# Two of sixteen query tiles of each unit folded inside the loop, three banks for maxima, four for scores

## What is computed

```python
q, k, v = (proj(wq, bq), proj(wk, bk), proj(wv, bv))      # 2 x 16 heads x 1024 x 8
scores = jnp.einsum('bhqd,bhkd->bhqk', q, k) * scale
attn = jax.nn.softmax(scores, axis=-1)
out = jnp.einsum('bhqk,bhkd->bhqd', attn, v)
...
x = layernorm(x + (out @ wo.T + bo));  x = layernorm(x + ffn(x))
```

## Time and profile before

| | |
|---|---|
| Runs | 442.76, 443.16, 443.18 us, median 443.16 |
| Profiled execution | span 441.5 us from first to last instruction |
| PE busy | 427.8 us (97%) |
| VectorE busy | 386.5 us (88%) |
| ScalarE busy | 367.7 us (83%) |
| GpSimd busy | 90.3 us (20%) |
| Granted PE clock | 1.000 on average |

### The profile page before, as it was taken

One profiled execution on the slowest core, in us unless ns is written; L12 is line 12 of the kernel. 1 busy time (PEld: TensorE's weight loads), 2 busy tenths in 40 slices (PEclk: granted clock), 3 DMA queues, 4 the chain that ended last, 5 costly groups with the idle time before them and its releaser, 6 DMA issues.

```text
span 441.5 us, 9824 instructions
## 1 busy us (share of the span) xinstructions
PE 427.8 (97%) x3496; PEld 227.0 (51%) x3498; DVE 386.5 (88%) x719; ACT 367.7 (83%) x694; POOL 90.3 (20%) x142
## 2 busy tenths in 40 slices
PE   8999999999999999999999999999899899999995
PEld 4543544444444444444444443544333488877884
DVE  6799999999999999999999999999884577657636
ACT  4487989998998999989899899999899886678762
POOL 9730000100000010000001002373311263046103
PEclk9999999999999999999999999999999999999999
DMA  6567741111130110113011001021021000000101
GB/s 165 176 196 129 270 147 33 44 28 28 48 122 25 45 31 28 27 48 122 25 46 33 26 27 49 14 43 47 15 39 50 13 8 1 1 2 2 48 1 48
DMA packets 17117, 24.88 MB, mean 56 GB/s; under 512 B 5169, under 2 KB 9009, under 8 KB 16689
## 3 DMA queue, kind: packets, MB, share of 16 engines
q1 hardware_dynamic: 16464, 23.68, 19.3%
q10 hardware_dynamic: 608, 0.59, 0.5%
HBM read 15.08 MB, written 7.60 MB: 51 GB/s over the span
## 4 chain that ended last, share of the span: by engine, by line
PE 76%; DVE 10%; ACT 5%; SPq 3%; DMA 2%; issue 2%; POOL 0%; POOLq 0%; DVEq 0%; ACTq 0%
PE ps L1369 24%; PE ps L1291 20%; PE ps L1479 16%; DVE negmax L977 9%; PE ps L1353 8%; ACT arena L664 2%; DMA parts_q<-arena 2%; PE ps L1223 2%; PE ps L1234 1%; PE ps L1423 1%; PE ps L1319 1%; PE ps L1263 1%; SPq L463 1%; SPq L435 1%; ACT v_pad L722 1%
## 5 line engine op out<-in xcount | busy, mean ns | idle before, releaser
L977 DVE TENSOR_REDUCE negmax<-ps 128x1 f32<-128x512 f32 x458 | 275.8, 701 | 1.8 <-PE ps L1291 1.5
L664 ACT ACTIVATE arena<-ps 128x512 f32<-128x512 f32 x360 | 190.0, 606 | 19.3 <-PE ps L1353 14.1
L1353 PE MATMUL ps<-qx,kx 64*128 64x512 f32 x512 | 171.3, 451 | 0.9 <-DMA qx<-mT 0.6
L1291 PE MATMUL ps<-kx,qx 61*128 61x512 f32 x468 | 160.2, 441 | 0.6 <-DMA qx<-parts_q 0.5
L1291 PEld LDWEIGHTS ps<-kx,qx 61*128 61x128 f32 x468 | 75.1, 184 | 88.6 <-DVE negmax L977 79.3
L1369 PE MATMUL ps<-arena,v_pad 128*32 128x256 f32 (+3 forms) x1328 | 104.8, 407 | 2.8 <-ACT arena L664 2.8
L664 ACT ACTIVATE hf<-ps 128x512 f32<-128x512 f32 x152 | 83.2, 604 | 9.4 <-PE ps L1353 8.4
L1353 PEld LDWEIGHTS ps<-qx,kx 64*128 64x128 f32 x512 | 78.9, 184 | 18.6 <-ACT arena L664 11.8
L1479 PE MATMUL ps<-hid,w_high 128*128 128x512 f32 (+1 forms) x296 | 68.3, 388 | 0.8 <-issue 0.4
L1479 PEld LDWEIGHTS ps<-hid,w_high 128*128 128x128 f32 x296 | 54.2, 188 | 12.3 <-issue 0.8
L1369 PEld LDWEIGHTS ps<-arena,v_pad 128*32 128x32 f32 x1328 | 28.5, 108 | 37.1 <-issue 30.7
(11 more groups left out here) (107 smaller groups left out, 317.2 us busy)
## 6 DMA issues: line engine op xcount, KB each, us to landing
qx<-parts_q SPq DMA_DIRECT2D x60, 64.0 KB, 2.1
late_sb<-in_late SPq DMA_DIRECT2D x3, 1280.0 KB, 5.5
kx<-parts_k SPq DMA_DIRECT2D x56, 64.0 KB, 2.2
parts_q<-prt SPq DMA_DIRECT2D x3, 512.0 KB, 6.4
parts_q<-arena SPq DMA_DIRECT2D x3, 512.0 KB, 8.3
xT_sb<-in_xT SPq DMA_DIRECT2D x4, 256.0 KB, 4.2
xT_sb<-arena SPq DMA_DIRECT2D x28, 32.0 KB
prt<-den SPq DMA_DIRECT2D x7, 128.0 KB
```

The costliest lines, as they stand in the source:

```text
L664: nc.scalar.activation(probs(n // HG)[:, heads(n), :], ps[:, PLAN["score", n][0], :], ACT.Exp, scale=SCALE).then_inc(exp_done, 1)
L977: nc.vector.tensor_reduce(negmax[:, t // TURNS % 2, m % 2, h * QT + q:h * QT + q + 1], ps[:, MAX_BANK + m % 4, :], AX.X, ALU.max, negate=T ...
L1291: nc.tensor.matmul(ps[:, half_bank(m), :], qx[at, slot, qc, h, q * P:(q + 1) * P], kx[at, slot, h, part * C:(part + 1) * C], start=True, s ...
L1353: nc.tensor.matmul(ps[:, bank, :], kx[at, slot, h % PAIR, kt * P:(kt + 1) * P], qx[at, slot, qc, h % PAIR, :], start=True, stop=True)\
```

## The change

In units 2 to 12, tiles 2 and 9 of 16 (`SPARED`) are folded as in the part before the loop. `max_plan` writes out VectorE's and PE's order. At a spared tile t the four places 2t, 2t+1, 2t+4, 2t+5 hold: the apart matmul (difference of keys) of t, the two halves of tile t + 2, and the folded half of t.

The apart matmul takes its bank from the scores' rotation, and ScalarE's `copy_spared` empties it. That rotation gets one bank more (bank 5; four rotate), and the maxima have one fewer (`LOOP_BANKS`, three). The differences are now needed for every head group: `d_dram` grows to `G_ALL` groups. SP stores batch 0's right after its k and q, and loads slot 1's in between the loads of q for that slot. Batch 1's differences are computed by GpSimd and ScalarE (`kd_late`), stored by SP after its waits for the stores of q, and SP waits for these stores before its loop. In the loop SP loads the differences with each unit pair's q. GpSimd also clears the unused rows of the two new slots ahead of the first `split_max`.

VectorE's loop over four units is written out. `larger` follows the second half of the next unit, where it followed the first.

```diff
+SPARED = (2, 9)
+SPARED_FROM, SPARED_TO = 2 * TURNS, 13 * TURNS
...
-FIRST_BANKS, LATE_BANKS = [7, 0, 6, 1], (4, 5)
+FIRST_BANKS, LATE_BANKS = [7, 0, 6, 5, 1], (4,)
 MAX_BANK = 2
+LOOP_BANKS = (4, 2, 3)
...
+def turn_ops(g):
     return range(AHEAD + RUN * g, min(AHEAD + RUN * (g + 1), 2 * U_ALL * TURNS)) if g < RUNS else range(0)
...
+
+def max_plan():
+
+    first, last = 2 * WHOLE, 2 * U_ALL * TURNS
+    ops = {j: ("half", j // 2, j % 2) for j in range(first, last)}
+    for t in range(SPARED_FROM, SPARED_TO):
+        if t % TURNS in SPARED:
+            ops.update(zip((2 * t, 2 * t + 1, 2 * t + 4, 2 * t + 5),
+                           (("apart", t, 1), ("half", t + 2, 0), ("half", t + 2, 1), ("folded", t, 0))))
+    bank, after, taken, count = {}, {}, {}, first
+    for j in range(first, last):
+        if ops[j][0] != "apart":
+            bank[j] = LOOP_BANKS[(count - first) % len(LOOP_BANKS)]
+            after[j] = count + 1 - len(LOOP_BANKS) if count >= first + len(LOOP_BANKS) else LEFT_BY[bank[j]]
+            count += 1
+            taken[j] = count
+    return ops, bank, after, taken
+
+
+OPS, OP_BANK, OP_AFTER, TAKEN = max_plan()
+TAKEN_ALL = max(TAKEN.values())
+APART = [j for j in OPS if OPS[j][0] == "apart"]
+FOLDS = [next(j for j in OPS if OPS[j][:2] == ("folded", OPS[a][1])) for a in APART]
+
+
+def first_of_unit(j):
+    return j % (2 * TURNS) == 0
+
+
+def first_late(j):
+
+    g0 = j // (2 * QC * TURNS) * (2 * QC * TURNS)
+    return (g0 >= 2 * PER * TURNS and OPS[j][::2] == ("half", 1)
+            and all(OPS[i][::2] != ("half", 1) for i in range(g0, j)))
+
+
+def first_apart(j):
+    return j in APART and all(a // (2 * QC * TURNS) != j // (2 * QC * TURNS) for a in APART[:APART.index(j)])
+
...
-    order, last, plan = FIRST_BANKS[:-1], {}, {}
+    order, plan = FIRST_BANKS[:-1], {}
...
-            place(("score", n))
+                last.update({bank: ("reduced", TAKEN_ALL) for bank in LATE_BANKS})
+            if n is not None:
+                place(("score", n))
         if g in TURN_AT and g >= RUNS:
             place(("max", TURN_AT[g]))
         w = unit_from(g)
...
         kd_part = [w_high[:, PAIR + j, :] for j in range(HALVES)]
+        kd_part_late = [w_high[:, 5 + j, :] for j in range(HALVES)]
...
+
         probs_2 = arena[1][:, 2 * U_ALL * C:].bitcast(F32).rearrange("p (s h c) -> p s h c", s=2, h=HG)
 
...
+
+                for j in range(HALVES):
+                    sp.dma_start(d_dram[b * NG + g0:b * NG + g1, :, :, j].rearrange("g h d t -> (g h d) t"),
+                                 parts[j][g0 * HG * DH:g1 * HG * DH, :]).then_inc(kd_stored, 16)
+
+            def load_kd(g, slot):
+
+                for r in range(2):
+                    for i in range(HALVES):
+                        at = r * GROUP + i * HALVES * DH
+                        src = d_dram[bass.ds(g, 1), r * PAIR:(r + 1) * PAIR].rearrange("o h d j t -> (o d j) h t")
+                        sp.dma_start(kd_slot[at:at + HALVES * DH, slot].bitcast(F32), src).then_inc(kd_rows[slot], 16)
+
             def load_max(i, w):
...
                 store_q(0, i, 1, NG, q_out[0])
+            sp.wait_ge(apart_low, 1)
...
+            sp.wait_ge(kd_stored, 16 * HALVES)
+            load_kd(1, 1)
...
+            sp.wait_ge(kd_late_low, 1)
+            store_kd(1, 0, NG, kd_part_late)
+            sp.wait_ge(kd_stored, 2 * 16 * HALVES)
...
+                    load_kd(g, slot)
                     sp.wait_ge(scores, base + KT * HG * 3 // 2)
                     load_k(g, slot, 0, C, rows_in[slot][0])
...
+                act.wait_ge(max_scores, APART[n] + 1)
+                if n < 2:
+                    act.wait_ge(max_taken, 2 * WHOLE)
+                else:
+                    act.wait_ge(max_taken, TAKEN[FOLDS[n - 2]])
+                nc.scalar.activation(spared_sb(n), ps[:, PLAN["apart", n][0], :], ACT.Relu).then_inc(over, 1)
+
             for t in range(FOLD, WHOLE):
...
+                for op, n in beside(g):
+                    if op in APART:
+                        copy_spared(APART.index(op))
+                    if n is None:
+                        continue
...
             pool.wait_ge(rows_set, 4)
+            for r in range(2):
+                nc.gpsimd.memset(kd_slot[r * GROUP + ROWS:(r + 1) * GROUP].bitcast(F32), 0.0).then_inc(kd_set, 1)
+                pool.wait_ge(kd_set, 3 + r)
             split_max(None, 0)
+            pool.wait_ge(proj_ready, 2)
+            nc.gpsimd.tensor_tensor(kd_gap, proj[:, 1, :], proj[:, 0, :], ALU.subtract).then_inc(kd_late, 1)
+            pool.wait_ge(kd_late_high, 1)
+            nc.gpsimd.tensor_tensor(half(kd_part_late[1]), kd_gap, kd_part_late[0], ALU.subtract)\
+              .then_inc(kd_late_low, 1)
...
+            def turn_op(j):
+
+                dve.wait_ge(max_scores, j + 1)
+                kind, t, part = OPS[j]
+                h, q = head_of(t)
+                if kind == "folded":
+                    n = FOLDS.index(j)
+                    dve.wait_ge(over, WHOLE - FOLD + n + 1)
+                    nc.vector.tensor_tensor_reduce(spared_sb(n), ps[:, OP_BANK[j], :], spared_sb(n),
+                                                   -1.0, 3.0e38, ALU.add, ALU.min,
+                                                   negmax[:, t // TURNS % 2, 0, h * QT + q:h * QT + q + 1])\
+                      .then_inc(max_taken, 1)
+                    return
+                nc.vector.tensor_reduce(negmax[:, t // TURNS % 2, part, h * QT + q:h * QT + q + 1],
+                                        ps[:, OP_BANK[j], :], AX.X, ALU.max, negate=True)\
                   .then_inc(max_taken, 1)
 
...
+            def turn_ops_of(j0, j1):
+                for j in range(j0, j1):
+                    if OPS[j][0] != "apart":
+                        turn_op(j)
+                    if j % (2 * TURNS) == 1:
+                        larger(j // (2 * TURNS) - 1)
...
+                slot, qc = g % 2, t // TURNS % QC
+                at, h, rows = rows_of(t)
+                if first_of_unit(j):
+
+                    pe.wait_ge(rows_in[slot][qc], (g // 2 + 1) * LOAD_INC[qc])
+                if first_late(j):
+
+                    pe.wait_ge(rows_late[slot], g // 2 * LOAD_INC[1])
+                if first_apart(j):
+
+                    pe.wait_ge(kd_set, 4)
+                    pe.wait_ge(kd_rows[slot], (g + slot) // 2 * LOAD_INC[1])
+                if kind == "apart":
+                    bank, prior = PLAN["apart", APART.index(j)]
+                    bank_free(prior)
+                    keys = kd_slot[at, slot, h, :]
+                else:
+
+                    bank = OP_BANK[j]
+                    pe.wait_ge(max_taken, OP_AFTER[j])
+                    keys = kx[at, slot, h, part * C:(part + 1) * C]
+                nc.tensor.matmul(ps[:, bank, :], rows, keys, start=True, stop=True)\
                   .then_inc(max_scores, 1)
...
+                elif kind == "apart":
+                    pe.wait_ge(over, WHOLE - FOLD + n + 1)
```

More of the change, by code:

```diff
@@ L23 @@
 from contextlib import ExitStack
+from itertools import zip_longest
 import concourse.bass as bass
@@ L127, in bank_plan @@
 def bank_plan():
-    order, last, plan = FIRST_BANKS[:-1], {}, {}
+    order, plan = FIRST_BANKS[:-1], {}
+    last = {bank: ("reduced", LEFT_BY[bank]) for bank in order if bank in LEFT_BY}
     held = FIRST_BANKS[-1]
@@ L141, in bank_plan @@
             place(("max", TURN_AT[g]))
-        for n in scores_of(g):
+        for op, n in beside(g):
+            if op in APART:
+                place(("apart", APART.index(op)))
             if n == TAIL * HG:
                 order[3:3] = LATE_BANKS
-                last.update({bank: ("reduced", 2 * U_ALL * TURNS) for bank in LATE_BANKS})
-            place(("score", n))
+                last.update({bank: ("reduced", TAKEN_ALL) for bank in LATE_BANKS})
+            if n is not None:
+                place(("score", n))
         if g in TURN_AT and g >= RUNS:
@@ L321, in build @@
         over = sem("over")
+        kd_late = sem("kd_late")
+        kd_late_high, kd_late_low = sem("kd_late_high"), sem("kd_late_low")
+        kd_stored = sem("kd_stored")
+        kd_rows = [sem(f"kd_rows{s}") for s in range(2)]
         proj_ready = sem("proj_ready")
@@ L997, in _ @@
             dve.wait_ge(max_split, 1)
-            def turn_halves_from(i, m0, m1):
-                for m in range(m0, m1):
-                    turn_half(i, m)
-                    if m % (2 * TURNS) == 0:
-                        larger(i, m // (2 * TURNS) - 1)
-            with dve.Fori(0, ITERS - 1) as i:
-                turn_halves_from(i, 2 * WHOLE, 2 * WHOLE + 2 * PER * TURNS)
+            def turn_ops_of(j0, j1):
[4 more added lines that the diff above has]
+                        larger(j // (2 * TURNS) - 1)
             def invert(n):
@@ L1284, in turn_half @@
-                if part == 0:
-                    if t == 0:
```

(31 more changed lines are left out.)

62 lines of the change are left out of this document (31 added, 31 removed).

## The result

Four executions of the changed kernel took 455.24 to 456.24 us, median 455.54, against 443.08 us (442.76 to 443.18) for the kernel before: a ratio of 1.0284, interval 1.0271 to 1.0297. It is 12.5 us slower. The forecast was 450.6 us, slower, in a range up to 453.5; the sign was right and the size too small.

A forecast was written before the change was run, and what follows sets the result against it. VectorE was taken to set the loop's pace, PE close behind; 5.3 us (SP's queue) + 0.6 (spared units) + 1.5 (units 13 to 15) = 7.4 us on 443.16 gave 450.6 us, range 444.5 to 453.5.

The forecast's parts named there:

- Bound: Steady loop: VectorE sets the pace at 1.79 us a group of three halves, PE close behind at 1.69.
- SP's queue before unit 1: Three things put ahead of the load of unit 1's maxima make PE wait 5.3 us (4.2 to 6.7).
- (a): SP's queue before unit 1: four loads of differences for slot 1, 256 KB, put at 1.7 us.
- (b): SP's queue before unit 1: two 256 KB stores after the waits for q; 3.6 us with (c).
- (c): SP's queue before unit 1: a wait until both stores have landed; 3.6 us together with (b).
- rival 4: Before unit 1: PE's idle 5.9 us lowers its clock, costing about 1.6 us: 452.2 us, chance 0.20.
- Spared units: Units 2 to 12: 19.27 us each against 19.22, +0.6 us over eleven units, bounds -1 to +2.
- The loop of the forecast: Three maxima banks: a group's third half waits for the previous group's third half, 3.70 us for two groups.
- Rival 1: Spared units: bank depth does not bind, units take 18.2 to 18.4 us: 438.5 us, chance 0.10.
- rival 2: Spared units: loop binds but late weights don't count, 3.59 us for two groups: 444.6 us, chance 0.14.
- Units 13 to 15: No spared tile but three maxima banks: 19.7 us each, together +1.5 us (0 to 2).
- VectorE's written-out loop: VectorE's loop: no gap where it turns back, so nothing to win, bounded by 0.2 us either way.

The follow-up runs named there:

- e5: Kernel before with VectorE's loop written out and `larger` one half later, banks as before, no tile spared, no added transfers: 442.95 us, ratio 1.0003.
- e3: Changed kernel with 20 extra unread matmuls ahead of PE's wait for unit 1's maxima, to keep PE busy: 454.48 us, ratio 1.0263.
- e4: Kernel before with three banks for maxima, four for scores, VectorE's loop written out, no tile spared, no added transfers: 452.02 us, ratio 1.0201.
- e2: Changed kernel with unit 1's maxima load issued ahead of SP's waits for the stores of k and q: 449.74 us, ratio 1.0134.
- e10: Changed kernel with unit 1's maxima loaded ahead of SP's waits and ScalarE's loop copies cut to 16 of 512 columns: 447.96 us, ratio 1.011.
- e6: Changed kernel with banks as before, four for maxima and three for scores, which apart matmuls share: 462.29 us, ratio 1.042.
- e7: Changed kernel with four banks for maxima, three for scores, and unit 1's maxima loaded ahead of SP's waits: 455.25 us, ratio 1.0269.
- e1: Changed kernel with unit 1's maxima load issued after the waits for q's stores but ahead of the late differences' stores: 450.81 us, ratio 1.018.
- e9: Changed kernel with four maxima banks, which apart matmuls share, three for scores, and unit 1's maxima loaded ahead of SP's waits: 450.97 us, ratio 1.0166.
- e11: As e9, but one spared tile a unit (tile 9) in place of two: 446.0 us, ratio 1.0077 against the kernel before.
- e8: Kernel before with only unit 1's maxima load moved ahead of SP's waits for the stores of k and q: 442.5 us, ratio 0.9994.

## Why the prediction was right and wrong

**Bound.** That VectorE sets the pace with PE close behind held: e5, with the old banks, has the old 19.22 us a unit, and its VectorE is again busy all the time.

**SP's queue before unit 1, 5.3 us.** Held, at 4.6: unit 1's first score starts at 60.95 in place of 56.37. (a) put at 1.7: the last of the small loads ends 53.79 in the changed kernel, and the first store of differences, behind the waits for q, goes out at 54.37; the load is 4.55 us late in all, of which the stores take 3.36, so some 1.2 are left for (a). How much of these 1.2 is the change and how much is chance is open, as SP's issues differ between executions (last section). (b) and (c), put at 3.6 (by size, the two rows of the forecast would rather have given 3.9), took 3.36. Batch 0's stores of differences, 2.69 us of issue at 29.28, also stand ahead of that load and are not in the forecast; they are hidden, as SP's next load comes at 33.35 in place of 33.21. The estimate by the Trainium skill, "DMA: Bandwidth & Descriptors", section "Anatomy of one DMA", was 3.1 us for that pair; the measurement lies between it and mine. That section is on DMAs that GpSimd issues, these are issued by SP, which the forecast does not say.

**The clock, rival 4.** This is one of the two steps that failed. It was given a chance of 0.20 and 1.6 us, and the sum was made without it. All four executions of the changed kernel have a mean clock of 0.991 or 0.992, and e3 prices the fall at 2.2 us. The 1.6 us came from filler matmuls at the start of the kernel, where the lower clock lasts as long as nine of them (and 3.62 - 1.9 is 1.7, not 1.6); here the lower clock lasted from 59.4 to 66.2 us, 5.3 us of it with work for PE, and VectorE and ScalarE had to fill up again behind it. The Trainium skill, "TensorE: Matmul & The Clock Gate", section "Part 1: The HAM clock gate", speaks of an idle array falling back to half rate; the trace agrees (0.50 from 59.4 us, within the wait of 5.3 us that began at 55.7), and by it I called rival 4 the likelier course and still made the sum without it.

**Spared units, 19.27 us.** This is the other step that failed, and by its size the larger. The loop of the forecast exists and has its size: 3.69 us a pair in the changed kernel and in e4. Rival 1 (depth does not bind) and rival 2 (late weights do not count) are excluded by it. The unit took 19.57 us. Over three units of e2, whose units take 19.59 us, group by group, PE's time over 1.69 us a group comes to 4.55 us: late third halves and their late weights 3.6 (put at 3.5), the turned maxima 0.54 (put at 0.2), and scores that wait for ScalarE 0.35 (put at 0). The last term is "ScalarE gets two copies, I cost them at nothing". The cover named there, ScalarE's 9.5% of idle time, is not a cover: a queue emptied late by 0.6 us delays the next exponentials whatever the average. By e10 the copies give 0.14 us a unit. The transposes are a slip of the sum: three units have three of them, 0.18 us each, and it put 0.2 us once; that is 0.11 us a unit. The remaining 0.05 us a unit are pairs somewhat longer than 3.70 us. Over eleven units this is +3.9 us where +0.6 stood, outside the -1 to +2 that the range used, though the bound named before it, +4 with ScalarE's backlog, has this size; the copies turned out to be half of the excess.

**Units 13 to 15.** Put at +1.5, measured +1.2; e4, with the same banks, has the same 59.7 us for them, and e5, with the old banks and VectorE's loop as in e4, has 57.9: by this pair it is +1.8. Both levels were off, and it cancels: the kernel before takes 19.5 us a unit there and not 19.22, the changed one 19.9 and not 19.7.

**VectorE's written-out loop.** Put at nothing; e5 says nothing too.

**What it adds up to.** Of the 12.1 us, SP's queue has 4.6, the clock 2.2, unit 2's maxima behind the first score of unit 1 0.5 (8.45 us in e3, 7.90 before), the ten spared units after it 3.6, the last units 1.2. Against the forecast's 7.4 the spared units are 3.5 too many, the clock 2.2, SP's queue 0.7 and the last units 0.3 too few. Neither miss alone would have carried the time above 453.5 us; both together did. That the sign was right owes nothing to them.

**Why folding can't be had here.** This I had not seen before the experiments. Folding with three banks for maxima gains 0.36 us a unit over none (19.57 against 19.93), but those three banks cost 0.71 (19.93 against 19.22). With four for maxima the scores have three, and units take 19.84 and 20.29 us, where without folding they take 19.22. Four for maxima, four for scores and one for products would be nine banks, and there are eight. My theory in e6 and e7, that depth of the maxima was the only obstacle, fell. Whether a shorter copy would make folding pay with these banks, and whether a fold whose difference needs no copy by ScalarE would pay, was not tried. No kernel here is measurably faster than the one before.

## What to carry to other kernels

Before a bank is moved from one rotation to another, follow the loop through the shallower one (matmul, reader, release, weights) and compare it with the slack that the pace leaves: here 0.06 us a group were missing, and it cost 9 us. A share of idle time is an average, and no cover by itself: ask how long the operations behind an added one can wait before another engine does. Where a change lets TensorE idle for microseconds, the fall of its clock belongs in the sum, priced from rows in which the other engines have to fill up again, not as a rival.

## What was not expected of the hardware

The clock's fall is not tied to a fixed wait in these runs. It came with a wait of 5.3 us in the changed kernel, of 1.9 us in e1 and of 1.3 us in e9, and did not come with one of 1.2 us in e2. PE's timeline in e9, then its busy time behind that wait:

```profile
57.97 0.68 PE L1489 MATMUL ps<-qx,kx 64*128 64x512 f32 x1 [1.30 <-DMA qx<-mT]
```

```profile
58.00:60.00 2.00, 2.00 (x9) 0.33 (x9) 0.00 (x0) 0.60 (x1) 0.00 (x0) 0.51 0.57 215
```

In e1 PE was back at work at 57.63 and the clock fell only at 58.96 (0.74 on average from 58 to 60), in e9 0.1 us after PE was back. It also differed between executions of one and the same kernel (e3: 0.997 to 0.998, once 0.992; e1: 0.992 to 0.998; e11: 0.998, twice 0.994). From unit 1's first score to `larger` a fall of 6.8 us cost 2.2 us in the changed kernel against e3 and 2.6 in e6 against e7, one of 3.4 us cost 1.4 in e1 against e3. What decides between these is open.

SP's issue of a DMA is not a constant: the same store of q took 0.92 us at 44.57 in the kernel before and 1.51 us at 47.31 in the changed one, a small load behind it 0.80 and 1.19, and the two stores of batch 0's differences 2.69 together, against 0.82 for the two of batch 1 at 54.37. The change is not needed for it: in e8, whose queue up to there is that of the kernel before, the same store took 1.71 us. The DMA engines were full around it (a share of 1.04 from 44 to 51 us), but they were also full while eight loads took 0.46 each (1.07 from 36 to 44 us), so that full engines alone are not the reason. It stays open.
